# A third SBUF home for projection chunks, loaded ahead of the last stores, and a projection start that waits for one PSUM bank pair at a time

## The chip, the cores and the metric

One core of a Trainium2 chip. A core has TensorE (PE, matrix products), VectorE (DVE), ScalarE (ACT), GpSimd (POOL) and SyncE (SP), which here issues nearly all DMA transfers, in one queue served by 16 DMA engines. The metric is the device time of one execution in microseconds (us), as a median of several.

## What is computed

Four layers in a row on x, of shape 256 x 256 x 64 (tokens by channels). Each layer adds to x the result of a normalised, gated, pairwise contraction:

```python
x = x + layer(_gn(x), ...)              # four times; _gn: group norm with 32 groups
# one layer:
xn = layernorm(x)
left, right = (xn @ Wl + bl) * sigmoid(xn @ Wlg + blg), (xn @ Wr + br) * sigmoid(xn @ Wrg + brg)
out = einsum('bikh,bjkh->bijh', left, right)    # layers 1 and 3 contract over the other axis
out = layernorm(out) * sigmoid(xn @ Wog + bog)  # layers 2 and 3 gate after the last product
return out @ Wo + bo
```

Layers 0 and 2 also multiply left and right by a mask; layer 0 keeps left and right in bf16.

## The kernel before

Layers are numbered 0 to 3. A layer is one block of code in which every engine runs its own list of instructions, and semaphores alone order them. Its stages are `prepare` (a few small products), `norm`, `project` for the first half of the channels, `contract` (`contract_low` in layer 0), `project` for the second half, `contract_kept`, and `finish`. Nothing but semaphores separates one stage from the next, so an engine goes on into the next stage when its own waits allow. SP's transfers are issued strictly in the order of its list: a wait in it holds back all that stands behind it.

**norm.** It handles x as 16 chunks (`NCH`) of 1 MB, two tiles each, so 32 tiles t. For each tile PE centres it into one of three PSUM bank pairs, `banks[t % 3]`, and takes the variance in `banks[3]`; ACT squares it and makes the reciprocal root (logarithm, exponential); DVE scales it (L712, semaphore `normed`) and splits it into a high and a low f16 part (L722, L724, semaphore `lows_ready`). SP stores both parts of chunk n to DRAM (tensor `XH`, or `XHA` in layers 1 and 3) with four transfers of 256 KB each; chunk 14 counts on `stored[0]`, chunk 15 on `stored[1]`.

**project.** It reads the normalised x back in another order, again as 16 chunks c0 to c15 of 1 MB (two transfers of 512 KB, `load_xh_chunk`, L303), and has four SBUF homes for them, one per chunk number modulo 4. All four lie in `kept0`. Home 2 shares its bytes with two of norm's scaled tiles (`yc`), home 3 with one of norm's input chunks; in the second half all four share them with the buffers from which `contract` stores its result. A chunk is handled in eight groups (masked layers 0 and 2) or four units (layers 1 and 3). PE projects into all eight PSUM banks in turn (L802; L812 and L817), ACT takes the sigmoid (L839; L850), in masked layers POOL and DVE multiply the gate by the mask (L865, L886), and DVE multiplies gate and value into the array `LR` (L893; L904, semaphore `products_ready`). PE may be eight groups ahead of DVE's products, not more. Since `LR` also holds the high parts of norm, DVE's first product of the first half waits until chunk 14 is stored:

```python
                if half == 0:
                    dve.wait_ge(stored[0].s, stored[0].n)
                    dve.wait_ge(stored[2].s, stored[2].n)
                    dve.wait_ge(lows_ready.s, lows_ready.n)
```

**contract.** PE contracts in four pieces of four groups; ACT copies each group out of PSUM (`copied`), and SP stores each finished piece to DRAM (tensor `OS`, 2 MB, L1081). Before the store of piece 3 it waits until that of piece 2 has landed, and then issues the second half's c0 and c1. c2 and c3 wait in `project` for the store of piece 3.

Of the kernel before, what the change touches and what calls it, by code (L numbers as in the profile page):

```python
# [48 lines left out]
P = 128  # L49
N = 256  # L50
C = 64
# [52 lines left out]
def build(nc, x_in, masks, consts, params, out):  # L104
    ctx = ExitStack()
    with ctx:
        def sb(name, shape, dt=F32):
            return ctx.enter_context(nc.sbuf_tensor(name, shape, dt))
# [19 lines left out]
        class Arena:  # L128
# [5 lines left out]
            def take(self, cols):  # L134
# [5 lines left out]
        kept0 = sb("kept0", [P, HALF * N])  # L140
        obuf = [kept0[:, i * 16 * 256:(i + 1) * 16 * 256] for i in range(2)]

        xh_b = [[obuf[h // 2][:, at:at + COLS // 2].bitcast(F16) for at in (h % 2 * COLS, h % 2 * COLS + COLS // 2)]
                for h in range(4)]
        squares = [sb(f"squares{i}", [P, 4 * N]) for i in range(2)]

        rings = [[sb(f"{name}s", [P, 2 * BANK])[:, :], square[:, :]] for name, square in zip(("sig", "msg"), squares)]
# [453 lines left out]
        def norm(block, number, layer):  # L601
# [12 lines left out]
            @block.sync  # L614
            def _(sp):
                def store(n, h):
                    sp.wait_ge(lows_ready.s, lows_ready.n + 2 * n + 2)
                    sp.sem_inc(tick.s, 1)
                    for part, v in enumerate((high[h], low[h])):
                        store_xh(sp, n, part, v, k_is_b, stored[h])  # L620

                for h in range(4):
                    sp.wait_ge(stored[h].s, stored[h].n)

                def store_entered(c):
                    sp.dma_start(pair_chunk(XT, c // 8, c % 8), entered(c)).then_inc(stored[2].s, 16)

                load_xt_chunk(sp, 2, 2)
                for n in range(NCH - 1):
                    if n + 3 < from_dram:  # L630
                        sp.wait_ge(centered.s, centered.n + 2 * n + 2)
                        load_xt_chunk(sp, n + 3, n % 3)
                    if n >= 1:
                        store(n - 1, (n - 1) % 2)
                    if from_dram <= n + 2 < NCH:
                        store_entered(n + 2)
                for h in range(2):
                    sp.wait_ge(stored[h].s, stored[h].n + per * (4 if k_is_b else 5))

                load_xh_chunk(sp, 0, 0, k_is_b)  # L640
                store(NCH - 2, 0)
                load_xh_chunk(sp, 1, 1, k_is_b)
                store(NCH - 1, 1)

            @block.tensor
            def _(pe):
                def center(t):
                    n, u = divmod(t, 2)
                    h = n % 3
                    if u == 0 and n < from_dram:  # L650
                        pe.wait_ge(loaded[h].s, loaded[h].n + 16 * (n // 3) + 16)
                    pe.wait_ge(normed.s, normed.n + t - 2)
                    for half in range(2):
                        for s in range(2):
                            rows = slice(C * s, C * s + C)
                            to = banks[t % 3][C * half:C * half + C, s * BANK:(s + 1) * BANK]
                            x = xa[h] if n < from_dram else entered(n)
                            if k_is_b:
                                cols = x[rows, (2 * half + u) * BANK:(2 * half + u + 1) * BANK]
                            else:  # L660
                                cols = x[rows, :].rearrange("p (g j r) -> p j g r", g=8, j=16)[
                                    :, 8 * half + 4 * u:8 * half + 4 * u + 4, :, :]
                            last = pe.matmul(to, cen[rows, rows], cols, start=True, stop=True)  # L663
                    last.then_inc(centered.s, 1)

                def vary(t):
                    pe.wait_ge(squared.s, squared.n + t + 1)
                    pe.wait_ge(logged.s, logged.n + t)
                    for u in range(2):
                        last = pe.matmul(banks[3][:, u * BANK:(u + 1) * BANK], K(K_MEAN),  # L670
                                         sq[t % 3][:, u * BANK:(u + 1) * BANK], start=True, stop=True)
                    last.then_inc(variance.s, 1)

                center(0)
                center(1)
                for t in range(tiles):
                    vary(t)
                    if t + 2 < tiles:
                        center(t + 2)

            @block.scalar
            def _(act):
                def square(t):
                    act.wait_ge(centered.s, centered.n + t + 1)
                    act.wait_ge(variance.s, variance.n + t - 2)
                    act.activation(sq[t % 3], banks[t % 3][:, :], ACT.Square, bias=cb).then_inc(squared.s, 1)  # L686

                def root(t):

# [17 lines left out]
            def _(dve):  # L707
                def scale(t):

                    dve.wait_ge(rooted.s, rooted.n + t + 1)  # L710
                    dve.wait_ge(lows_ready.s, lows_ready.n + t - 3)
                    dve.scalar_tensor_tensor(yc[t % 4], banks[t % 3][:, :], cb, rs[t % 3], ALU.add, ALU.mult).then_inc(normed.s, 1)  # L712

                def halve(t):

# [22 lines left out]
        def project(block, number, layer, half):  # L738
# [21 lines left out]
            def _(sp):  # L760

                if half == 1:
                    sp.wait_ge(stored[1].s, stored[1].n)
                    sp.wait_ge(summed.s, summed.n)
                for h in range(4 if half == 1 and layer["low"] else 2, 4):
                    load_xh_chunk(sp, h, h, k_is_b)
                if half == 0:
                    for h in range(3):
# [7 lines left out]

            @block.tensor
            def _(pe):
                if half == 0:
                    pe.wait_ge(normed.s, normed.n)  # L780
                    pe.wait_ge(logged.s, logged.n)
                else:
                    pe.wait_ge(copied.s, copied.n)
                    pe.wait_ge(copied_v.s, copied_v.n)
                    pe.wait_ge(sums_taken.s, sums_taken.n)
# [8 lines left out]
                with pe.Fori(0, NCH // 4) as i:  # L794
                    for h in range(4):
                        pe.wait_ge(landed[h].s, landed[h].n + 32 * i + 32)
                        if masked:
                            for g in range(8):
                                pe.wait_ge(products_ready.s, products_ready.n + 32 * i + 8 * h + g - 7)
                                for j in range(4):  # L800
                                    for part, w in enumerate((whigh, wlow)):
# [5 lines left out]
                        for two in range(2):  # L807
                            for q in (2 * two, 2 * two + 1):
                                unit = 16 * i + 4 * h + q
                                pe.wait_ge(products_ready.s, products_ready.n + unit - 3)  # L810
                                for s, j in sides_last:
                                    pe.matmul(bank(2 * q + s)[:, j * P:(j + 1) * P], tokens(h, s, q, j, slice(0, P)),  # L812
                                              whigh[:, half * P:(half + 1) * P], start=j == 0, stop=False)
# [165 lines left out]
        def contract(block, number, layer):  # L979
# [89 lines left out]
            def _(sp):  # L1069
                if more:  # L1070
                    load_parameters(sp, number + 1)
                for piece in range(4):
                    ut, cq = divmod(piece, 2)
                    if piece == 3:
# [3 lines left out]
                        for h in range(2):  # L1078
                            load_xh_chunk(sp, h, h, layer["k_is_b"])
                    sp.wait_ge(copied.s, copied.n + 4 * (piece + 1))  # L1080
                    sp.dma_start(OS[ut, :, :, cq, :].rearrange("v p f -> p v f"),  # L1081
                                 hold[piece % 2].rearrange("p (v f) -> p v f", v=16)) \
                        .then_inc(stored[piece % 2].s, 16)
# [684 lines left out]
```

## Time and profile before

| | us |
|---|---|
| median of 3 runs | 2152.24 (2147.28 to 2158.65) |
| profiled execution, time | 2150.95 |
| profiled execution, span | 2148.8 |
| PE busy | 1888.1 (88%) |
| DVE busy | 1693.6 (79%) |
| ACT busy | 1591.5 (74%) |
| POOL busy | 595.4 (28%) |

The span runs from the first to the last instruction in the trace; the time is 2.15 us longer. Busy shares are means over stages with different limits: where an edit touches one place, what counts is which engine or transfer the others wait for at that place. PE's clock has two levels, shown as a granted clock of 1.00 (2.4 GHz) or 0.5 (1.2 GHz).

### The profile page before, as it was taken

To read this page: it belongs to the slowest core of one execution; us is meant where nothing else is said; L and a number is where in the kernel's file an instruction comes from. 1 tells how busy PE (TensorE), PEld (TensorE's weight loads), DVE (VectorE), ACT (ScalarE), POOL (GpSimd) and SP (SyncE) were. 2 spreads that over 40 slices of the span, in tenths; PEclk is the share of its full clock that TensorE was granted. 3 is DMA by queue.
4 is the path that set the end of the run, shared out by engine and by line. 5 is a ranking of instruction groups with operands and counts; after the bars stand their busy time and mean duration, and the time that the engine had idled before them with its cause. 6 is when DMAs were issued, how large, how long until landed. Compare 5 with 4: busy or idle time off the path is not lost. (4 is left out here: it accounts for less than half of the span.)

```text
span 2148.8 us, 44715 instructions
## 1 busy us (share of the span) xinstructions
PE 1888.1 (88%) x14485; PEld 1280.8 (60%) x14492; DVE 1693.6 (79%) x2690; ACT 1591.5 (74%) x2204; POOL 595.4 (28%) x574
## 2 busy tenths in 40 slices
PE   5687979699897998989989799899997879899998
PEld 4423959455422786855622697886552258777665
DVE  6798989989598877688969887878776977677665
ACT  3598969679897756569989775766888966566666
POOL 0001918175100000026400470732870000000755
PEclk8899989999999999999999999999999999999999
DMA  9589938279798739169979954917997993753897
GB/s 393 195 274 312 264 79 235 94 290 384 270 302 275 277 117 312 41 245 402 410 261 316 265 145 150 278 43 278 407 393 256 308 303 130 245 186 127 320 350 299
DMA packets 297397, 549.53 MB, mean 256 GB/s; under 512 B 14768, under 2 KB 170416, under 8 KB 273712
## 3 DMA queue, kind: packets, MB, share of 16 engines
q1 hardware_dynamic: 295680, 538.38, 72.9%
q10 hardware_dynamic: 1584, 9.51, 1.1%
q8 instruction: 68, 1.11, 0.2%
q14 instruction: 65, 0.53, 0.1%
HBM read 371.67 MB, written 176.16 MB: 255 GB/s over the span
## 5 line engine op out<-in xcount | busy, mean ns | idle before, releaser
L1603 POOL TENSOR_TENSOR LR<-LR 128x512 f32<-128x512 f32 x128 | 187.9, 1488 | 523.3 <-DVE LR L1649 501.2
L802 PE MATMUL bank<-whigh,kept 128*128 128x128 f16 x2048 | 268.2, 231 | 30.5 <-DMA kept<-XH 22.5
L1594 POOL TENSOR_TENSOR LR<-LR,sum 128x2048 f32<-128x2048 f32 x30 | 136.5, 4549 | 526.4 <-DVE LR L1408 526.4
L802 PEld LDWEIGHTS bank<-whigh,kept 128*128 128x128 f16 x2048 | 261.5, 150 | 34.6 <-issue 26.3
L802 PE MATMUL bank<-wlow,kept 128*128 128x128 f16 x2048 | 267.4, 230 | 0.0
L802 PEld LDWEIGHTS bank<-wlow,kept 128*128 128x128 f16 x2048 | 261.9, 150 | 0.0
L670 PE MATMUL bank<-LR,kst 128*128 128x512 f32 x512 | 254.3, 619 | 8.3 <-ACT LR L692 6.3
L865 POOL TENSOR_TENSOR msgs<-sigs,mask_sb 128x256 f32<-128x256 f32 x192 | 124.6, 663 | 487.1 <-ACT sigs L839 481.9
L1497 PEld LDWEIGHTS bank<-kst,LR 128*128 128x128 f32 x1024 | 151.0, 192 | 109.9 <-issue 90.7
L1509 PE MATMUL bank<-LR,wog 128*128 128x512 f16 x768 | 211.9, 385 | 4.8 <-ACT msgs L1550 4.0
L670 PEld LDWEIGHTS bank<-LR,kst 128*128 128x128 f32 x512 | 87.6, 191 | 179.1 <-issue 172.9
L812 PE MATMUL bank<-whigh,kept 128*128 128x128 f16 x2048 | 153.4, 226 | 37.1 <-DMA kept<-XHA 32.7
L1007 PE MATMUL bank<-LR 128*128 128x256 f32 x768 | 172.7, 387 | 7.0 <-DVE LR L904 4.2
L1263 PE MATMUL bank<-LR 128*128 128x256 f32 x768 | 169.9, 385 | 7.0 <-DVE LR L904 4.2
L1497 PE MATMUL bank<-kst,LR 128*128 128x128 f32 x1024 | 159.3, 279 | 14.7 <-ACT sigs L1545 7.7
L1007 PEld LDWEIGHTS bank<-LR 128*128 128x128 f32 x768 | 148.6, 194 | 28.3 <-DVE LR L904 4.6
L1263 PEld LDWEIGHTS bank<-LR 128*128 128x128 f32 x768 | 148.0, 193 | 28.2 <-DVE LR L904 4.6
L692 ACT ACTIVATE LR<-bank,epsx 128x1024 f32<-128x1024 f32 x128 | 142.9, 1116 | 25.7 <-PE bank L670 21.6
L812 PEld LDWEIGHTS bank<-whigh,kept 128*128 128x128 f16 x2048 | 121.1, 101 | 64.5 <-issue 36.3
L686 ACT ACTIVATE LR<-bank,small 128x1024 f32<-128x1024 f32 x128 | 140.8, 1100 | 16.5 <-PE bank L663 16.5
L839 ACT ACTIVATE sigs<-bank,small 128x256 f32<-128x256 f32 x256 | 121.1, 478 | 31.8 <-PE bank L802 25.4
L696 ACT ACTIVATE LR<-LR 128x1024 f32<-128x1024 f32 x128 | 135.5, 1058 | 4.0
(189 smaller groups left out, 4106.1 us busy)
## 6 DMA issues: line engine op xcount, KB each, us to landing
LR<-XT SPq DMA_DIRECT2D x103, 1024.0 KB, 8.9
kept<-XH SPq DMA_DIRECT2D x128, 512.0 KB, 5.8
kept<-XHA SPq DMA_DIRECT2D x128, 512.0 KB, 5.1
XT<-LR SPq DMA_DIRECT2D x56, 1024.0 KB, 9.0
LR<-XH SPq DMA_DIRECT2D x64, 512.0 KB, 6.7
LR<-XHA SPq DMA_DIRECT2D x64, 512.0 KB, 6.0
OS<-kept SPq DMA_DIRECT2D x12, 2048.0 KB, 7.5
LR<-OS SPq DMA_DIRECT2D x48, 512.0 KB, 8.5
```

The costliest lines, as they stand in the source:

```text
L670: last = pe.matmul(banks[3][:, u * BANK:(u + 1) * BANK], K(K_MEAN), sq[t % 3][:, u * BANK:(u + 1) * BANK], start=True, stop=True)
L686: act.activation(sq[t % 3], banks[t % 3][:, :], ACT.Square, bias=cb).then_inc(squared.s, 1)
L692: act.activation(lnv[t % 2], banks[3][:, :], ACT.Ln, bias=epsx[:, :], scale=1.0 / X_SCALE ** 2).then_inc(logged.s, 1)
L696: act.activation(rs[t % 3], lnv[t % 2], ACT.Exp, scale=-0.5).then_inc(rooted.s, 1)
L802: last = pe.matmul(bank(g)[:, j * P:(j + 1) * P], tokens(h, g // 4, g % 4, j, slice(0, P)), w[:, half * P:(half + 1) * P], start=part == 0 ...
L812: pe.matmul(bank(2 * q + s)[:, j * P:(j + 1) * P], tokens(h, s, q, j, slice(0, P)), whigh[:, half * P:(half + 1) * P], start=j == 0, stop= ...
L1007: last = pe.matmul(banks[e % 3][:, c * N:(c + 1) * N], src[:, kt, off_a + ch, ut * P:(ut + 1) * P], src[:, kt, off_b + ch, :], start=kt == ...
L1263: last = pe.matmul(banks[e % 3][:, c * N:(c + 1) * N], src[:, kt, off_a + 4 * g + c, ut * P:(ut + 1) * P], src[:, kt, off_b + 4 * g + c, : ...
L1497: last = pe.transpose(by_token(turn_bank(t))[:, :, j, :], n_t[c % len(nrm)][:, :, 4 * q + j], K(K_IDENT))
L1509: last = pe.matmul(bank(2 + t % 2), wog[w][:, :], pair_cols(x, q) if k_is_b else by_b(x, q), start=(w, part) == (0, 0), stop=w == 1)
L1594: pool.tensor_tensor(v, v, token(sum2, c, C), ALU.mult).then_inc(normalized.s, 1)
L1603: pool.tensor_tensor(by_b(x_of(c), q) if end else by_token_cols(x_of(c), q), by_token(gated[t % 4]), by_token_cols(xi[c % len(xi)], q), AL ...
```

## The change

`kept0` keeps homes 0, 1 and 3, and home 2 becomes a buffer of its own, `third_home`, of 8 KB per partition. The room comes from the region set aside for descriptors of dynamic DMAs, which is cut to 1024 bytes per partition. Home 3 takes the bytes that home 2 had.

- At the end of norm, the loads of c0, c1 and c2 are all issued before the stores of chunks 14 and 15. Before, c0 went ahead of the store of chunk 14, c1 between the two stores, and c2 and c3 behind both.
- In contract, c2 of the second half is loaded just before the store of piece 2. c3 alone is left for the place where c2 and c3 stood.
- norm's tiles use `banks[(t + 1) % 3]`, so that the last three tiles end in pairs 0, 1 and 2 in that order, and PE's first projections wait for one pair each (`norm_left`) and no longer for all of norm.

```diff
-        xh_b = [[obuf[h // 2][:, at:at + COLS // 2].bitcast(F16) for at in (h % 2 * COLS, h % 2 * COLS + COLS // 2)]
-                for h in range(4)]
+        xh_homes = [obuf[0][:, 0:COLS], obuf[0][:, COLS:2 * COLS], sb("third_home", [P, COLS])[:, :], obuf[1][:, 0:COLS]]
+        xh_b = [[v[:, at:at + COLS // 2].bitcast(F16) for at in (0, COLS // 2)] for v in xh_homes]
...
-                load_xh_chunk(sp, 0, 0, k_is_b)
+                for h in range(3):
+                    load_xh_chunk(sp, h, h, k_is_b)
                 store(NCH - 2, 0)
-                load_xh_chunk(sp, 1, 1, k_is_b)
                 store(NCH - 1, 1)
...
-                            to = banks[t % 3][C * half:C * half + C, s * BANK:(s + 1) * BANK]
+                            to = banks[(t + 1) % 3][C * half:C * half + C, s * BANK:(s + 1) * BANK]
...
-                for h in range(4 if half == 1 and layer["low"] else 2, 4):
+                for h in range(4 if half == 1 and layer["low"] else 3, 4):
                     load_xh_chunk(sp, h, h, k_is_b)
...
-                if half == 0:
-                    pe.wait_ge(normed.s, normed.n)
-                    pe.wait_ge(logged.s, logged.n)
-                else:
+                def norm_left(h, two_banks):
+                    if half == 0 and h == 0:
+                        if two_banks < 3:
+                            pe.wait_ge(normed.s, normed.n - 2 + two_banks)
+                        else:
+                            pe.wait_ge(logged.s, logged.n)
...
+                                if g % 2 == 0:
+                                    norm_left(h, g // 2)
                                 pe.wait_ge(products_ready.s, products_ready.n + 32 * i + 8 * h + g - 7)
...
                     sp.wait_ge(copied.s, copied.n + 4 * (piece + 1))
+                    if piece == 2:
+                        load_xh_chunk(sp, 2, 2, layer["k_is_b"])
                     sp.dma_start(OS[ut, :, :, cq, :].rearrange("v p f -> p v f"),
...
-    nc = bacc.Bacc("TRN2", target_bir_lowering=False, num_devices=1)
+    nc = bacc.Bacc("TRN2", target_bir_lowering=False, num_devices=1, dynamic_dma_scratch_size=1024)
```

SP's list at the end of norm and the start of the first projection in layer 0, before (`XH<-LR` is the store of chunk 14, `XH<-sum` that of chunk 15, `kept<-XH` a load of half a chunk):

```order
L303 DMA kept<-XH 128x8x256 x2
L277 DMA XH<-LR 64x2x1024 x4
L303 DMA kept<-XH 128x8x256 x2
L277 DMA XH<-sum 64x2x1024 x4
L759 UNCONDITIONAL_BRANCH
L303 DMA kept<-XH 128x8x256 x4
```

The same place after the change:

```order
L303 DMA kept<-XH 128x8x256 x4
L303 DMA third_home<-XH 128x8x256 x2
L277 DMA XH<-LR 64x2x1024 x4
L277 DMA XH<-sum 64x2x1024 x4
L759 UNCONDITIONAL_BRANCH
L303 DMA kept<-XH 128x8x256 x2
```

Four transfers, c1 and c2, moved ahead of the store of chunk 14; the same happens in the other three layers.

SP's list in contract of layer 1, before (`OS<-kept` is the store of a piece):

```order
L1081 DMA OS<-kept 128x16x256 x3
L303 DMA kept<-XHA 128x2x1024 x4
L1081 DMA OS<-kept 128x16x256
L759 UNCONDITIONAL_BRANCH
L303 DMA kept<-XHA 128x2x1024 x4
```

The same place after the change:

```order
L1090 DMA OS<-kept 128x16x256 x2
L303 DMA third_home<-XHA 128x2x1024 x2
L1090 DMA OS<-kept 128x16x256
L303 DMA kept<-XHA 128x2x1024 x4
L1090 DMA OS<-kept 128x16x256
L759 UNCONDITIONAL_BRANCH
L303 DMA kept<-XHA 128x2x1024 x2
```

c2 moved from behind the store of piece 3 to ahead of the store of piece 2.

DVE's list where the first projection of layer 0 begins, before; it is the same after, 7 lines further down in the file:

```order
L724 SCALAR_TENSOR_TENSOR sum<-kept,sum 128x2x512 [waits highs_ready]
L869 UNCONDITIONAL_BRANCH
L876 UNCONDITIONAL_BRANCH [waits lows_ready,stored2,stored0]
L876 ISA
L885 REGISTER_ALU [waits gates_ready]
L886 ISA [waits products_ready]
L886 TENSOR_TENSOR msgs<-sigs,mask_sb 128x256
```

Nothing moved here: the wait for `stored0` still stands ahead of all of DVE's work in the projection.

## Rows read from the trace of the kernel before

**Rows 1.** Waits of PE: line, releaser, total us, times, longest.

```profile
PE bank L812 <- DMA kept<-XHA: 32.7, 7, 7.7
PE bank L802 <- DMA kept<-XH: 22.5, 5, 6.8
```

**Rows 2.** Timeline, norm into projection, layer 0: start, duration, engine, [idle before <- releaser].

```profile
195.95 2.12 SPq L303 DMA_DIRECT2D kept<-XH  x2
...
199.43 3.14 SPq L277 DMA_DIRECT2D XH<-LR  x4
...
199.45 1.28 DVE L712 SCALAR_TENSOR_TENSOR kept<-bank,small,LR 128x1024 f32<-128x1024 f32 x1
...
202.86 0.33 PE L802 MATMUL bank<-whigh,kept 128*128 128x128 f16 x1 [5.69 <-DMA kept<-XH]
202.98 0.31 PE L802 MATMUL bank<-wlow,kept 128*128 128x128 f16 x1
...
206.25 0.42 DVE L886 TENSOR_TENSOR msgs<-sigs,mask_sb 128x256 f32<-128x256 f32 x1 [1.80 <-ACT sigs L839]
...
216.81 0.28 PE L802 MATMUL bank<-whigh,kept 128*128 128x128 f16 x1 [2.69 <-DMA kept<-XH]
...
218.80 0.43 DVE L886 TENSOR_TENSOR msgs<-sigs,mask_sb 128x256 f32<-128x256 f32 x1 [2.58 <-ACT sigs L839]
```

**Rows 3.** Windows: us, busy PE, PEld, DVE, ACT, POOL, PEclk, DMA share, GB/s.

```profile
203.00:217.00 14.00, 10.86 (x131) 10.60 (x132) 9.89 (x22) 7.64 (x16) 7.27 (x12) 0.80 1.01 308
...
224.00:270.00 46.00, 46.00 (x736) 46.00 (x735) 45.66 (x114) 43.80 (x93) 44.17 (x69) 1.00 0.97 249
704.00:745.00 41.00, 40.73 (x792) 33.13 (x787) 34.79 (x51) 31.50 (x50) 0.00 (x0) 1.00 0.90 311
...
830.00:850.00 20.00, 19.95 (x389) 16.28 (x386) 16.89 (x24) 14.96 (x25) 0.00 (x0) 1.00 0.99 352
```

**Rows 4.** Timeline, norm into projection, layer 1.

```profile
690.82 1.41 DVE L904 SCALAR_TENSOR_TENSOR LR<-bank,small,sigs 128x512 f32 x2 [1.37 <-DMA XHA<-LR]
...
695.75 1.89 PE L812 MATMUL bank<-whigh,kept 128*128 128x128 f16 x16 [4.23 <-DMA kept<-XHA]
...
701.05 1.06 PE L812 MATMUL bank<-whigh,kept 128*128 128x128 f16 x16
```

**Rows 5.** Timeline of DVE, first projection of layer 2: first of c0, first of c3.

```profile
1205.89 0.42 DVE L886 TENSOR_TENSOR msgs<-sigs,mask_sb 128x256 f32<-128x256 f32 x1 [2.78 <-ACT sigs L839]
...
1222.73 0.41 DVE L886 TENSOR_TENSOR msgs<-sigs,mask_sb 128x256 f32<-128x256 f32 x1
```

**Rows 6.** Timelines of SP and PE, contract into second projection, layer 1.

```profile
806.21 2.54 SPq L303 DMA_DIRECT2D kept<-XHA  x4
...
821.09 5.91 SPq L303 DMA_DIRECT2D kept<-XHA  x8
...
812.82 1.06 PE L812 MATMUL bank<-whigh,kept 128*128 128x128 f16 x16 [1.42 <-ACT kept L1021]
...
826.66 1.89 PE L812 MATMUL bank<-whigh,kept 128*128 128x128 f16 x16 [6.92 <-DMA kept<-XHA]
...
831.23 1.07 PE L812 MATMUL bank<-whigh,kept 128*128 128x128 f16 x16
...
834.54 1.06 PE L812 MATMUL bank<-whigh,kept 128*128 128x128 f16 x16
```

**Rows 7.** Timelines of SP, PE and DVE, second projection, layer 2.

```profile
1350.89 6.19 SPq L303 DMA_DIRECT2D kept<-XH  x5
...
1357.39 0.33 PE L802 MATMUL bank<-whigh,kept 128*128 128x128 f16 x1 [6.53 <-DMA kept<-XH]
...
1360.09 0.42 DVE L886 TENSOR_TENSOR msgs<-sigs,mask_sb 128x256 f32<-128x256 f32 x1 [6.51 <-ACT sigs L839]
...
1365.64 0.41 DVE L886 TENSOR_TENSOR msgs<-sigs,mask_sb 128x256 f32<-128x256 f32 x1
...
1370.02 0.86 DVE L886 TENSOR_TENSOR msgs<-sigs,mask_sb 128x256 f32<-128x256 f32 x1 [0.28 <-DVE LR L893]
```

More of the change, by code:

```diff
@@ L685, in square @@
                     act.wait_ge(variance.s, variance.n + t - 2)
-                    act.activation(sq[t % 3], banks[t % 3][:, :], ACT.Square, bias=cb).then_inc(squared.s, 1)
+                    act.activation(sq[t % 3], banks[(t + 1) % 3][:, :], ACT.Square, bias=cb).then_inc(squared.s, 1)
                 def root(t):
@@ L711, in scale @@
                     dve.wait_ge(lows_ready.s, lows_ready.n + t - 3)
-                    dve.scalar_tensor_tensor(yc[t % 4], banks[t % 3][:, :], cb, rs[t % 3], ALU.add, ALU.mult).then_inc(normed.s, 1)
+                    dve.scalar_tensor_tensor(yc[t % 4], banks[(t + 1) % 3][:, :], cb, rs[t % 3], ALU.add, ALU.mult).then_inc(normed.s, 1)
                 def halve(t):
@@ L778, in _ @@
             def _(pe):
-                if half == 0:
-                    pe.wait_ge(normed.s, normed.n)
-                    pe.wait_ge(logged.s, logged.n)
-                else:
+                def norm_left(h, two_banks):
[4 more added lines that the diff above has]
+                            pe.wait_ge(logged.s, logged.n)
+                if half == 1:
                     pe.wait_ge(copied.s, copied.n)
@@ L809, in _ @@
                                 unit = 16 * i + 4 * h + q
+                                norm_left(h, q)
                                 pe.wait_ge(products_ready.s, products_ready.n + unit - 3)
```

## The prediction

> **What bounds the kernel now.** I read the waits of PE first, since PE is busy 88% of the span. In two lines PE waits for a chunk of the projection to land: 32.7 us in 7 waits and 22.5 us in 5 [rows 1]. I then looked in the timeline at where these twelve stand. All are in the first few chunks of a projection; further on there are none. There the pace is DVE's in masked layers (45.66 us busy of 46.00, for 736 / 64 = 11.5 chunks, so 4.0 us a chunk) and PE's in the others (40.73 of 41.00) [rows 3]. A projection therefore ends late by what its first chunks lose, and nothing later wins it back. The change touches two sorts of place: the start of the first half's projection (four layers) and of the second half's (layers 1 to 3; layer 0 loads all four chunks ahead already).
>
> The reader is to see one more thing. Where these waits stand, the DMA engines are never idle: share 1.01 at 308 GB/s over the first 14 us of layer 0's projection [rows 3]. Transfers that are issued sooner do not add room there. They only change places with others. So I ask, for each place, who is served later.
>
> **First projection, layer 0.** PE starts c0 at 202.86, when c0 lands (wait of 5.69 us); norm's last L712 began at 199.45 and took 1.28, so it was over at 200.73 [rows 2]. The waits for norm are thus covered by 2.1 us of waiting for c0, whose load keeps its place in SP's list. Waiting for one bank pair at a time gives 0; it would give up to 2.1 us if c0 came sooner, which nothing here brings about. The new order of banks moves no work.
>
> DVE's list has the wait for `stored0` (chunk 14) ahead of everything. In layer 1 the trace names it: DVE's first product, at 690.82, had waited 1.37 us for the store XHA<-LR [rows 4]. In layer 0 the store's four transfers are issued from 199.43 for 3.14 us and DVE starts at 206.25 [rows 2]; the row blames ACT, but it is 3.7 us after the last issue, and I take it to be the same wait. After the change the loads of c1 and c2 stand ahead of that store. Each is 2 x 512 KB = 1.05 MB; at 308 GB/s that is 3.4 us, together 6.8 us. SP's own time to issue them (2.12 us for a chunk [rows 2]) lies beside that. So DVE starts at 206.25 + 6.8 = 213.05. Behind that wait are queued all of DVE's products, behind them PE from the ninth group on (it may be eight ahead), and ACT behind PE. DVE has two chunks to do before c2: 213.05 + 2 x 4.0 = 221.1. Today it starts c2 at 218.80, because c2 landed only for PE's start at 216.81, a wait of 2.69 [rows 2]. The wait for c2 goes, the wait for the store takes its place, and the layer loses **2.3 us**. What is late next is c3: the bytes ahead of it are the same as before, so it lands where it did, one chunk's data behind c2 (about 216.81 + 3.4 = 220.2), and that is before DVE needs it at 225.
>
> **First projection, layer 2.** Same code: 1205.89 + 6.8 + 3 x 4.0 = 1224.7 for the first of c3, against 1222.73 [rows 5]: **+2.0**.
>
> **Layers 1 and 3.** The chunks are read at 352 GB/s [rows 3], 3.0 us each, so DVE starts at 690.82 + 6.0 = 696.8. PE's c1 needs the first product of c0, half of 1.41 us later: 697.5. Today c1 starts when it lands, at 695.75, after a wait of 4.23 [rows 4]. Loss **1.8 us**. c2 starts today with no wait at 701.05, so no further stall is saved. Layer 3 has the same instructions, and I take 1.8 again.
>
> **Second projection, layer 1.** The load of c2 goes ahead of the store of piece 2, and c0 and c1 are issued only when that store has landed: at 806.21 now, at 806.21 + 3.0 = 809.2 then. From issue to PE's start a chunk takes 826.66 - 821.09 = 5.57 us [rows 6], so PE starts c0 at 814.8 and not at 812.82. The long idle time brings the low clock, at which a chunk takes 831.23 - 826.66 = 4.57 us, against 834.54 - 831.23 = 3.31 [rows 6]: PE is through c0, c1 and c2 at 814.8 + 4.57 + 2 x 3.31 = 826.0. The store of piece 3 has the load's 3.0 us ahead of it too, so c3 is issued at 824.1 and starts at 829.7, after a wait of 3.7 us. It starts today at 831.23. But c3 now meets the low clock that c2 met: c4 starts at 829.7 + 4.57 = 834.2 against 834.54. The gain is **0.3 us**, out of a wait of 6.92: the bytes that must land before c3 are the same. Layer 3 (the wait of 7.7 in rows 1): 0.3 again.
>
> **Second projection, layer 2.** Here a chunk load is 3.4 us: c3 is issued at 1350.89 + 3.4 and PE starts it 1357.39 - 1350.89 = 6.5 us later, at 1360.8. DVE follows PE by 1360.09 - 1357.39 = 2.7 us and its first chunk takes 1365.64 - 1360.09 = 5.55 us at the low clock, so c4's first comes at 1369.0, against 1370.02 [rows 7]: gain **1.0 us**.
>
> **The other edits.** The buffer of its own and the smaller scratch region move no instruction, and no transfer here is issued by GpSimd: 0. The four waits of `norm_left` sit in a loop, so they are met in each of its 4 passes; in layers 1 and 3, where PE sets the pace, these are 32. No row has such a wait. PE's instructions start 0.12 us apart at the low clock [rows 2], which bounds it at 32 x 0.12 = 3.8 us; I take 0, since these are no matrix work and PE's queue runs ahead of its array.
>
> **Sum.** 2.3 + 2.0 + 1.8 + 1.8 - 0.3 - 0.3 - 1.0 = **+6.3 us**. Against the profiled execution's own time that is 2150.95 + 6.3 = 2157.3; it lies 1.3 below the median of the runs, and I give the time against the median: **2158.5**.
>
> The price on which all rests is how late two loads make the store. The break-even is a slip of 218.80 - 8.0 - 206.25 = 4.5 us in layer 0 and 695.75 - 0.7 - 690.82 = 4.2 in layer 1; I have 6.8 and 6.0. The slip is bounded below by 0 (the store overtakes) and above by two chunks at 249 GB/s [rows 3], 8.4 us, which adds 1.6 us in layers 0 and 2 and 2.4 in layers 1 and 3: +14.3 in all. In the second projections the low clock may stay away; then layers 1 and 3 gain 4.57 - 3.31 = 1.3 more each and layer 2 5.55 - 4.0 = 1.5 more, and the sum is +2.2.
>
> [...]
>
> **Rivals.**
> - *The low clock takes more (slower).* In layer 0 PE will be through the 64 products of c0 at 202.86 + 64 x 0.12 = 210.5 and idle until DVE's first product at 213.5, 3 us, and much the same in the other first projections. Waits of this size have brought the low clock here (rows 3: granted 0.80 over those 14 us). For layers 0 and 2 I left it out, because DVE has eight groups in hand. If it lasts over c1 and c2, each costs 1.55 more in masked layers (2 x 2 x 1.55 = 6.2) and c2 costs 1.26 more in each of the others (2.5): 6.3 + 8.7 = +15, 2167. It decides (over +10.8) when half of it comes true. Against it: 0.80 over 14 us is 5.6 us at the low level, which c0 alone fills today. 0.17.
> - *The loads and the store share (no change, or a little less).* If store and loads are served side by side and the slip is that of one load, 3.4 or 3.0 us: layer 0 206.25 + 3.4 + 8.0 = 217.65 (-1.1), layer 2 -1.4, layers 1 and 3 690.82 + 3.0 + 0.7 = 694.5 (-1.2 each), with -1.6 in the second projections: -6.5, 2145.7. For it: SP has only one queue but 16 engines, and a transfer waits on the slowest of them. Against it: the engines are full, so sharing makes both late. 0.17.
> - *The change does what it says (faster).* The loads cost nobody anything. First projections: 206.25 + 8.0 = 214.25 (-4.5), 1205.89 + 12.0 = 1217.9 (-4.8), 691.5 for 695.75 (-4.2, twice); second: c3 lands for 826.66, so -3.3 twice, and 1365.64 for 1370.02 (-4.4). Sum -28.7: 2123.5. It needs idle DMA engines, and the rows show none. 0.08.
> - *My forecast:* 0.58, with its own range of 2153 to 2164.
>
> **From these to the numbers.** What a measurement of this kernel can tell from no change is about 0.5%, 10.8 us: below 2141.5 is faster, above 2163.0 slower. Faster: 0.07 of the last rival and a little of the second, 0.09. Slower: 0.14 of the first, 0.06 of the forecast's upper bound, 0.20. Same: 0.71. The range leaves out the fast rival and the outer part of the low-clock one: 2144 to 2168.
>
> **What would show it.** Right: PE's wait at c2 of the first projections is gone; DVE's first product comes about 7 us (layers 0 and 2) and 6 us (1 and 3) later after the end of norm, held by the store of chunk 14; PE waits for DVE at c1. In contract, SP issues c0 and c1 3 us later after the store of piece 2; PE waits about 2 us more at c0, not at c2, and some 3.7 us at c3. PE's c0 in the first projections still waits for its chunk. Wrong: if DVE's first product keeps its distance to norm's end, the slip does not exist and the kernel is faster; if chunks c1 and c2 run at a granted clock of 0.5, it is slower than I say.

## The result, and the profile after

The changed kernel takes **2164.01 us** (median of 5 runs, 2160.9 to 2168.06), the kernel before 2152.24 (2147.28 to 2158.65, now 5 runs). The ratio is 1.0053, with a 95% interval of 1.0032 to 1.0073. So it is 11.4 us slower (from 6.9 to 15.7), where +6.3 was forecast. In the text below a difference is always (ratio - 1) times the median of the kernel before in the same comparison.

The page of the changed kernel, top (engine, busy us, share of the span, instructions) and bytes:

```profile
span 2161.9 us, 44727 instructions
...
PE 1887.9 (87%) x14485; PEld 1281.6 (59%) x14492; DVE 1689.6 (78%) x2690; ACT 1588.7 (73%) x2204; POOL 591.6 (27%) x574
...
DMA packets 297397, 549.53 MB, mean 254 GB/s; under 512 B 14768, under 2 KB 170416, under 8 KB 273712
```

The busy times are those of before within 4 us. No engine has more work; the time went into waits. PE's waits in the projection (line, releaser, total us, times, longest), which answer to [rows 1]:

```profile
PE bank L819 <- DMA kept<-XHA: 29.6, 6, 5.4
...
PE bank L808 <- DMA kept<-XH: 16.8, 3, 6.4
PE bank L808 <- DVE LR L900: 13.5, 6, 5.8
PE bank L819 <- DVE LR L911: 12.3, 3, 6.5
```

Waits for a chunk fell from 55.2 to 46.4 us. Waits for DVE's products, which were 3.7 us in all before, are now 25.8. Nearly all of these stand at c1 of the first projections (5.66, 5.47, 5.77 and 6.50 us in layers 0 to 3).

**First projection, layer 0.** SP, DVE and PE in the timeline (start, duration, engine, [idle before <- releaser]); compare [rows 2]:

```profile
195.54 5.19 SPq L303 DMA_DIRECT2D kept<-XH  x4
200.77 3.68 SPq L303 DMA_DIRECT2D third_home<-XH  x2
204.56 4.28 SPq L277 DMA_DIRECT2D XH<-LR  x4
...
198.89 1.28 DVE L712 SCALAR_TENSOR_TENSOR kept<-bank,small,LR 128x1024 f32<-128x1024 f32 x1
...
213.86 0.43 DVE L893 TENSOR_TENSOR msgs<-sigs,mask_sb 128x256 f32<-128x256 f32 x1 [9.96 <-DMA XH<-LR]
...
202.98 0.32 PE L808 MATMUL bank<-whigh,kept 128*128 128x128 f16 x1 [6.36 <-DMA kept<-XH]
...
214.74 0.32 PE L808 MATMUL bank<-whigh,kept 128*128 128x128 f16 x1 [5.66 <-DVE LR L900]
...
222.22 0.42 DVE L893 TENSOR_TENSOR msgs<-sigs,mask_sb 128x256 f32<-128x256 f32 x1
```

Count from the start of norm's last L712, since the whole trace is shifted by what comes earlier. The store of chunk 14 (`XH<-LR`) is issued 5.67 us after it, where before it was 0.02 us ahead. DVE's first product comes 14.97 us after it, before 6.80: a slip of 8.2 us, and the row now names the store itself. PE still waits for c0's chunk (6.36 us), so waiting for one bank pair at a time won nothing. PE then fills its eight groups and stands 5.66 us for DVE. DVE reaches c2 at 23.33 after L712, before at 19.35 (218.80 - 199.45).

**Layer 1**, the same place:

```profile
691.05 1.28 DVE L712 SCALAR_TENSOR_TENSOR kept<-bank,small,LR 128x1024 f32<-128x1024 f32 x1
...
704.24 1.41 DVE L911 SCALAR_TENSOR_TENSOR LR<-bank,small,sigs 128x512 f32 x2 [8.19 <-DMA XHA<-LR]
...
705.05 1.89 PE L819 MATMUL bank<-whigh,kept 128*128 128x128 f16 x16 [5.47 <-DVE LR L911]
...
710.11 1.07 PE L819 MATMUL bank<-whigh,third_home 128*128 128x128 f16 x16
```

DVE's wait of 1.37 us for the store [rows 4] has become 8.19, and PE's wait of 4.23 us at c1 for its chunk has become one of 5.47 us for DVE. DVE's first product comes 13.19 us after L712 (before 6.38), 14.24 in layer 2 (7.79) and 13.80 in layer 3 (6.63): slips of 6.8, 6.5 and 7.2 us.

**Second projection, layer 1.** Two rows of before that [rows 6] did not need, the start of contract and the stores of pieces 2 and 3:

```profile
749.54 14.08 PE L1007 MATMUL bank<-LR 128*128 128x256 f32 x64 [2.11 <-DVE LR L904]
...
798.68 0.36 SPq L1081 DMA_DIRECT2D OS<-kept  x1
...
812.49 0.37 SPq L1081 DMA_DIRECT2D OS<-kept  x1
```

The same of the changed kernel:

```profile
758.72 14.08 PE L1014 MATMUL bank<-LR 128*128 128x256 f32 x64 [2.11 <-DVE LR L911]
...
807.84 1.23 SPq L303 DMA_DIRECT2D third_home<-XHA  x2
809.12 0.60 SPq L1090 DMA_DIRECT2D OS<-kept  x1
819.73 2.51 SPq L303 DMA_DIRECT2D kept<-XHA  x4
822.28 0.61 SPq L1090 DMA_DIRECT2D OS<-kept  x1
835.46 4.60 SPq L303 DMA_DIRECT2D kept<-XHA  x6
...
825.56 1.89 PE L819 MATMUL bank<-whigh,kept 128*128 128x128 f16 x16 [4.99 <-DMA kept<-XHA]
...
841.87 1.88 PE L819 MATMUL bank<-whigh,kept 128*128 128x128 f16 x16 [4.65 <-DMA kept<-XHA]
...
846.82 1.06 PE L819 MATMUL bank<-whigh,kept 128*128 128x128 f16 x16
```

Counted from the start of contract (749.54, 758.72), with what the prediction's times come to on the same count (its 809.2, 814.8, 824.1, 829.7 and 834.2 less 749.54):

| us from the start of contract | before | predicted | after |
|---|---|---|---|
| store of piece 2 issued | 49.14 | - | 50.40 |
| it has landed: c0, c1 issued | 56.67 | 59.7 | 61.01 |
| PE starts c0 | 63.28 | 65.3 | 66.84 |
| store of piece 3 issued | 62.95 | - | 63.56 |
| it has landed: c3 issued | 71.55 | 74.6 | 76.74 |
| PE starts c3 | 81.69 | 80.2 | 83.15 |
| PE starts c4 | 85.00 | 84.7 | 88.10 |

The reader is to see two things. The store of piece 2 takes 10.61 us from its issue until SP goes on, before 7.53. That is 3.1 more, the 3.0 forecast. But it is also issued 1.26 us later, since SP first issues the two halves of c2 (1.23 us). And the store of piece 3 takes 13.18 us, before 8.60: it now follows c0 and c1 after 2.55 us, before after 6.28, so most of the data of two chunks is still ahead of it. Over the three layers, SP's own waits for these stores rise from 28.5 us (6 waits, the longest 5.8) to 54.8 (6, 11.1).

### The profile page after: what moved, and what is told of

Same layout as the page of the kernel before. It is cut to its first block and busy times, and to the rows that moved or that the text cites. A ratio compares the mean times of both kernels' runs of the same rounds, so it can differ in the third digit from the quotient of the medians.

```text
span 2161.9 us, 44727 instructions
## 1 busy us (share of the span) xinstructions
PE 1887.9 (87%) x14485; PEld 1281.6 (59%) x14492; DVE 1689.6 (78%) x2690; ACT 1588.7 (73%) x2204; POOL 591.6 (27%) x574
## 5 line engine op out<-in xcount | busy, mean ns | idle before, releaser
L808 PE MATMUL bank<-whigh,kept 128*128 128x128 f16 x1536 | 205.7, 233 | 33.5 <-DMA kept<-XH 16.8
L808 PEld LDWEIGHTS bank<-whigh,kept 128*128 128x128 f16 x1536 | 197.7, 150 | 37.3 <-issue 22.6
L808 PE MATMUL bank<-wlow,kept 128*128 128x128 f16 x1536 | 205.0, 232 | 0.0
L808 PEld LDWEIGHTS bank<-wlow,kept 128*128 128x128 f16 x1536 | 198.2, 150 | 0.0
L819 PE MATMUL bank<-whigh,kept 128*128 128x128 f16 x1536 | 120.2, 233 | 43.1 <-DMA kept<-XHA 29.6
L911 DVE SCALAR_TENSOR_TENSOR LR<-bank,small,sigs 128x512 f32 x128 | 90.2, 747 | 57.0 <-ACT sigs L857 39.6
```

Source lines behind the costliest of these rows:

```text
L808: last = pe.matmul(bank(g)[:, j * P:(j + 1) * P], tokens(h, g // 4, g % 4, j, slice(0, P)), w[:, half * P:(half + 1) * P], start=part == 0 ...
```

## The experiments

Nine kernels ran. Theory 1 in all: a store that something waits for is late by the loads issued ahead of it. The rival: the loads cost nothing there, and the time is lost to the low clock or to the new bank order and its waits. All results together (runs of the kernel before in the same comparison: 5 for the change, 11 to 24 for the others):

| run | norm's list | load of c2 in contract | median us | ratio (95%) | difference |
|---|---|---|---|---|---|
| the change | c0 c1 c2 s14 s15 | ahead of store of piece 2 | 2164.01 | 1.0053 (1.0032-1.0073) | +11.4 |
| e1_norm_side | c0 c1 c2 s14 s15 | behind store of piece 3, as before | 2159.88 | 1.0036 (1.0023-1.0049) | +7.7 |
| e2_contract_side | c0 s14 c1 s15 c2 | ahead of store of piece 2 | 2154.99 | 1.0013 (1.0000-1.0025) | +2.8 |
| e6_bank_pairs | c0 s14 c1 s15 c2 | as before | 2153.38 | 1.0001 (0.9991-1.0011) | +0.2 |
| e5_early_c2 | c0 s14 c1 s15 c2 | right behind store of piece 1 | 2143.39 | 0.9961 (0.9948-0.9974) | -8.4 |
| e3_two_after_store | c0 s14 c1 c2 s15 | as before | 2152.00 | 0.9997 (0.9986-1.0008) | -0.6 |
| e4_one_ahead | c0 c1 s14 c2 s15 | as before | 2144.06 | 0.9965 (0.9952-0.9978) | -7.5 |
| e7_both | c0 s14 c1 c2 s15 | right behind store of piece 1 | 2140.71 | 0.9940 (0.9919-0.9961) | -12.9 |
| e9_earlier_c2 | c0 s14 c1 s15 c2 | right behind store of piece 0 | 2141.34 | 0.9947 (0.9927-0.9966) | -11.4 |
| e8_one_ahead_early | c0 c1 s14 c2 s15 | right behind store of piece 1 | 2133.83 | 0.9913 (0.9898-0.9929) | -18.7 |

(s14, s15: stores of chunks 14 and 15. All of these have the third home, the smaller scratch and the rotated banks.)

**e1_norm_side** keeps the change's norm and undoes its contract.

```diff
-                    if piece == 2:
-                        load_xh_chunk(sp, 2, 2, layer["k_is_b"])
...
-                for h in range(4 if half == 1 and layer["low"] else 3, 4):
+                for h in range(4 if half == 1 and layer["low"] else 2 if half == 1 else 3, 4):
```

> The changed kernel with its contract side undone: c0, c1 and c2 of the first projection are still loaded ahead of the stores of chunks 14 and 15, but in contract c2 stands where it stood before, behind the store of piece 3. Store-slip theory: all of the loss of the first projections stays. VectorE's first product comes 13 to 15 us after the start of norm's last scaling (6.4 to 7.8 before), and the kernel is some 10 us slower than before, about 2162. Rival, that the loss is that of the second projections' new order: no slower than before, 2152.

Measured +7.7 us, between +4.9 and +10.5. In layer 0 DVE's first product again waits for the store (start of L712 and first product):

```profile
199.26 1.28 DVE L712 SCALAR_TENSOR_TENSOR kept<-bank,small,LR 128x1024 f32<-128x1024 f32 x1
...
214.72 0.43 DVE L893 TENSOR_TENSOR msgs<-sigs,mask_sb 128x256 f32<-128x256 f32 x1 [10.45 <-DMA XH<-LR]
```

That is 15.46 us after L712. The norm side is most of the loss.

**e2_contract_side** keeps the change's contract and has norm's list as before.

```diff
-                for h in range(3):
-                    load_xh_chunk(sp, h, h, k_is_b)
+                load_xh_chunk(sp, 0, 0, k_is_b)
                 store(NCH - 2, 0)
+                load_xh_chunk(sp, 1, 1, k_is_b)
                 store(NCH - 1, 1)
+                load_xh_chunk(sp, 2, 2, k_is_b)
```

> The changed kernel with its norm side undone: c0, store of 14, c1, store of 15, c2 as before, while in contract c2 is loaded ahead of the store of piece 2. The prediction's term for this side was -1.6 us. By the trace of the changed kernel it is +2.5: the store of piece 2 lands 4.3 us later for layers 1 and 3 (not 3.0), TensorE waits about 5 us at c0 and about 4.5 at c3 of the second projections, and the kernel takes about 2155. If the loads really cost nobody, it is 10 us faster.

Measured +2.8 us (0 to +5.4). Its two halves, 7.7 + 2.8 = 10.5, make up the change's 11.4 within the intervals. In layer 1 SP's list shows the same gaps as in the changed kernel, 10.35 us from the store of piece 2 to c0 and 12.78 from the store of piece 3 to c3:

```profile
805.03 1.23 SPq L303 DMA_DIRECT2D third_home<-XHA  x2
806.30 0.60 SPq L1091 DMA_DIRECT2D OS<-kept  x1
816.65 2.51 SPq L303 DMA_DIRECT2D kept<-XHA  x4
819.21 0.61 SPq L1091 DMA_DIRECT2D OS<-kept  x1
831.99 5.30 SPq L303 DMA_DIRECT2D kept<-XHA  x6
```

**e6_bank_pairs** has both lists of before, and so only the third home, the smaller scratch, the rotated banks and the waits of `norm_left`. Its diff is that of e1 and e2 together.

> Only the buffer of its own, the smaller scratch region, the turned bank order and the waits for one bank pair each; every transfer in its old place. Theory: nothing waits for norm there, since c0 lands 2 us after norm's last scaling, so 0, within 2 us of the kernel before. Rival (the 16 passes with extra waits on TensorE, or the new place of a buffer, cost): several us slower, up to the whole 11.8.

Measured +0.2 us (-1.9 to +2.4). These edits cost nothing and bring nothing, the repeated waits of `norm_left` (bounded at 3.8 us in the prediction) included.

**e5_early_c2** has norm as before, and moves contract's load of c2 from behind the wait for piece 2's copies to ahead of it. SP then issues it right behind the store of piece 1.

```diff
+                    if piece == 2:
+                        load_xh_chunk(sp, 2, 2, layer["k_is_b"])
                     sp.wait_ge(copied.s, copied.n + 4 * (piece + 1))
-                    if piece == 2:
-                        load_xh_chunk(sp, 2, 2, layer["k_is_b"])
```

> As the kernel with only the contract side, but c2 of the second projection is issued one wait sooner, right behind the store of piece 1, where the DMA engines go idle before piece 2 is ready. Theory (what costs is the load's place ahead of a store that is waited for): the store of piece 2 lands 7.5 us after its issue as before, c0 starts as before, c3 is issued directly behind the store of piece 3, TensorE waits about 4 us at c3, and each of the three layers gains 3 to 4.5 us: about 2142. Rival (a low clock and a wait at c3 take the gain back, wherever c2 stands): within 3 us of the kernel before.

Measured -8.4 us: from e2, two lines swapped, and 11.2 us. Layer 1, contract's start, SP, and PE at c0, c3 and c4:

```profile
752.87 13.43 PE L1015 MATMUL bank<-LR 128*128 128x256 f32 x61 [2.11 <-DVE LR L912]
...
786.47 0.37 SPq L1091 DMA_DIRECT2D OS<-kept  x1
786.88 3.38 SPq L303 DMA_DIRECT2D third_home<-XHA  x2
801.99 0.37 SPq L1091 DMA_DIRECT2D OS<-kept  x1
809.53 2.51 SPq L303 DMA_DIRECT2D kept<-XHA  x4
815.80 0.36 SPq L1091 DMA_DIRECT2D OS<-kept  x1
824.35 4.60 SPq L303 DMA_DIRECT2D kept<-XHA  x6
...
816.10 1.06 PE L820 MATMUL bank<-whigh,kept 128*128 128x128 f16 x16 [1.39 <-ACT kept L1029]
...
829.85 1.80 PE L820 MATMUL bank<-whigh,kept 128*128 128x128 f16 x16 [3.55 <-DMA kept<-XHA]
...
834.52 1.06 PE L820 MATMUL bank<-whigh,kept 128*128 128x128 f16 x16
```

The stores take 7.54 and 8.55 us until SP goes on, as before the change (7.53 and 8.60). PE starts c0 as soon as contract's last copy is made (the releaser is ACT, as before), c3 at 76.98 after contract's start where before it was 81.69, and c4 at 81.65 where before it was 85.00. So a home for a third chunk is worth something; it was the place in the list that lost it.

**e9_earlier_c2** issues that load one piece earlier still (`if piece == 1`), right behind the store of piece 0.

> The norm side is as in the kernel before. In the contract section the load of c2 is issued ahead of the wait for piece 1's copies, right behind the store of piece 0, one piece earlier than in the run with the early load. Theory 1 (what the load gains there is only that it is out of the way of the store of piece 2; once it is, earlier is no better): same as that run, -8.4 us, 2143, give or take 2. Theory 2 (how far ahead of the store of piece 2 the load stands still decides, because the transfers between are slow): -11 or better. Theory 3 (it now delays the store of piece 1, which the copies of piece 3 wait for, since the two stores share a buffer): it gives back 3 us or more at the end of contract, -5 or less.

Measured -11.4 us. The intervals of e5 and e9 overlap, so whether the extra 3 us are real, and with it the choice between theories 1 and 2, stays open. Theory 3 (the store of piece 1 becomes the next victim) falls: in layer 1 that store is issued at 787.56, 18 us behind the load (769.56), and for the last 7.5 of them the DMA engines are idle (share 0.01 over 780 to 787.5).

**e3_two_after_store** has contract as before and puts c1 and c2 between the two stores of norm.

```diff
-                for h in range(3):
-                    load_xh_chunk(sp, h, h, k_is_b)
+                load_xh_chunk(sp, 0, 0, k_is_b)
                 store(NCH - 2, 0)
+                load_xh_chunk(sp, 1, 1, k_is_b)
+                load_xh_chunk(sp, 2, 2, k_is_b)
                 store(NCH - 1, 1)
```

> Norm side only, with the order c0, store of 14, c1, c2, store of 15; contract as before. The store that VectorE waits for keeps its place, and c2 overtakes only the store of 15, for which nobody waits in the first three chunks. Store-slip theory: VectorE's first product 6.4 to 7.8 us after the start of norm's last scaling, as in the kernel before; c2 lands some 3 us sooner, and layers 0, 2 and 3 gain 1.5 to 3 us each: about 2144 to 2148. Rival (the store of 15 is also waited for, by the loads from c4 on, and they come late instead): within 2 us of the kernel before.

Measured -0.6 us (-3.0 to +1.7): a miss. The store that DVE waits for is not delayed (DVE waits 1.53 us for it in layer 1, before 1.37), and PE has no wait of 1 us or more for c2 in the first projections, but PE's wait for c1 is still there in layer 1, and behind it c1 runs at the low clock:

```profile
695.75 1.88 PE L820 MATMUL bank<-whigh,kept 128*128 128x128 f16 x16 [3.95 <-DMA kept<-XHA]
...
700.96 1.07 PE L820 MATMUL bank<-whigh,third_home 128*128 128x128 f16 x16
```

```profile
695.70:701.00 5.30, 5.25 (x65) 4.57 (x66) 1.41 (x2) 1.42 (x3) 0.00 (x0) 0.55 1.05 403
```

(The second fence is the window over c1, with the columns of [rows 3].) In layer 1 of the kernel before, in the trace of [rows 4], c2 had no wait that could be won back. New waits also stand at c3: 1.72 us in layer 0 (for DVE) and 1.49 in layer 2 (for the chunk).

**e4_one_ahead** has contract as before and puts only c1 ahead of the store of chunk 14.

```diff
-                for h in range(3):
-                    load_xh_chunk(sp, h, h, k_is_b)
+                load_xh_chunk(sp, 0, 0, k_is_b)
+                load_xh_chunk(sp, 1, 1, k_is_b)
                 store(NCH - 2, 0)
+                load_xh_chunk(sp, 2, 2, k_is_b)
                 store(NCH - 1, 1)
```

> Norm side only, with one load more ahead of the store of 14 instead of two: c0, c1, store of 14, c2, store of 15. Store-slip theory: the slip is half of that of the change, 3 to 4 us (VectorE's first product 10 to 11.5 us after the start of norm's last scaling), which is just under the break-even of 4.5 and 4.2 us, so the time is near the kernel before, -3 to +2 us. If the loss grows with the number of moved loads and not with a threshold, it is half of what two loads cost, +4 us: 2156.

Measured -7.5 us (-10.3 to -4.7), better than either theory had it. DVE's first product slips by 4.2, 3.0, 3.2 and 2.7 us in the four layers (10.96, 9.38, 11.00 and 9.30 after L712), so one load costs half of what two do, and each slip stays below the break-even of 4.5 or 4.2 us that the prediction worked out. In layer 1 PE's waits at c1 fall from 4.23 to 1.31 us, and c1 then runs at the full clock:

```profile
689.38 1.28 DVE L713 SCALAR_TENSOR_TENSOR kept<-bank,small,LR 128x1024 f32<-128x1024 f32 x1
...
698.76 1.41 DVE L912 SCALAR_TENSOR_TENSOR LR<-bank,small,sigs 128x512 f32 x2 [4.38 <-DMA XHA<-LR]
...
699.57 1.28 PE L820 MATMUL bank<-whigh,kept 128*128 128x128 f16 x16 [1.31 <-DVE LR L912]
...
702.88 1.28 PE L820 MATMUL bank<-whigh,third_home 128*128 128x128 f16 x16
```

```profile
699.50:704.50 5.00, 4.86 (x96) 4.00 (x96) 4.29 (x8) 2.54 (x4) 0.00 (x0) 1.00 1.05 397
```

c1 takes 3.31 us from start to start, in e3 5.21 and in the change 5.06. The profiled execution of e3 took 2144.72 us and that of e4 2151.72, the other way round from their medians, so the traces show the places and the medians the totals.

**e7_both** is e3's norm with e5's contract.

> Both orders that keep clear of a store that is waited for: c0, store of 14, c1, c2, store of 15 at the end of norm, and c2 of the second projection issued right behind the store of piece 1. If the two are independent, the gains add: 8.4 us of the early c2 and 4 to 8 of the other, about 2136 to 2140. If both give the same wait back to something later (a pace that another engine sets), less than either sum: above 2142.

Measured -12.9 us (-17.4 to -8.4). The time, 2140.71, lies between the two that were expected. e3's -0.6 and e5's -8.4 make -9.0: they add up within the interval, though only just.

**e8_one_ahead_early** is e4's norm with e5's contract.

> The norm side of the run with one load ahead (c0, c1, store of chunk 14, c2, store of chunk 15), which alone gave -7.5 us, and the contract side of the run with the early load of c2 (issued right behind the store of piece 1, before the wait for the copies of piece 2), which alone gave -8.4. They lie at different places of the program. Theory 1 (a place gains what its own first waits lose, and places add up): -7.5 - 8.4 = -15.9 us, 2136, ratio 0.9926. Theory 2 (the pace of DVE or PE in the rest of the projection takes part of it back): no better than the better of the two, about -9, 2143. Between the two, at -12.5, neither is borne out. In the profile under theory 1: DVE's first product about 3 us later after norm than in the kernel before, no wait of PE at c2 of the first projections, and no wait of over 2 us at c3 of the second ones.

Measured -18.7 us (-22.0 to -15.3), where adding gives -15.9 and theory 2 about -9. The places add up. One sign did not come: PE was to wait no more than 2 us at c3 of the second projections, and it waits 3.45 us in layer 1 and 3.79 in layer 3 (1.86 in layer 2), as in e5 (3.55 in layer 1). This kernel beats both others: 2133.83 us, with the same bytes and the same work.

## Why the prediction was right or wrong

The time lies in the range (2144 to 2168) and at the upper edge of the forecast's own (2153 to 2164). At +11.4 us it is just over the 10.8 from which the prediction speaks of "slower" (it gave that 0.20, and 0.71 to "no change"); the interval, 6.9 to 15.7, reaches to both sides. The direction, the places and the mechanism of the first projections came as forecast. One term, that of the second projections, had the wrong sign: -1.6 us forecast, +2.8 to +4.4 measured.

To see which, one must not compare single executions alone: a stretch of the same code differs by 2 to 4 us between two of them. So I took, from the profiled execution of each kernel, two stretches per layer: from the last L712 to contract's first matmul (the first projection), and from that to the first matmul of the second half's contract (the second projection). The mean of the kernels with the old list is set against those with the change's list and the better ones:

| stretch | layer 0 | layer 1 | layer 2 | layer 3 | sum of differences |
|---|---|---|---|---|---|
| first projection, list of before (5 kernels) | 78.6 | 66.1 | 78.0 | 66.2 | |
| change's list (2: the change, e1) | +2.0 | +1.9 | +1.4 | +2.0 | +7.2 |
| c0 s14 c1 c2 s15 (2: e3, e7) | -1.4 | -0.5 | -0.7 | -1.0 | -3.6 |
| c0 c1 s14 c2 s15 (2: e4, e8) | -1.3 | -2.3 | -0.2 | -2.0 | -5.9 |
| second projection, list of before (5) | | 127.6 | 141.0 | 122.2 | |
| change's list (2: the change, e2) | | +3.8 | -2.2 | +2.8 | +4.4 |
| c2 early (4: e5, e7, e8, e9) | | -3.1 | -6.3 | -3.4 | -12.8 |

**First projections (+7.9 forecast): the mechanism right, the number with some luck.** +7.2 in the table, +7.7 in e1. DVE's `stored0` wait took the place of c2's, PE waits for DVE at c1, and c0's chunk still starts the projection. The slips (8.2, 6.8, 6.5, 7.2) are in three layers larger than the forecast ones (6.8, 6.0, 6.8, 6.0). In layer 0 it all but reaches the upper bound of 8.4: SP's issuing does not lie beside the data as I had it, for the six loads take 5.19 + 3.68 = 8.87 us to issue where c0's two took 2.12, and the store is issued behind that. Against the one trace that I costed from, the four stretches of the changed kernel grew by 3.8, 2.6, 1.9 and 2.6 us, 10.8 in all, about what the larger slips give (7.9 + 3.0). That trace is 4.0 us shorter in these stretches than the mean of the five (in layer 0 76.61, mean 78.6), and only so does 7.2 come out beside 7.9: that nearness is luck. Nor does "c2 starts today with no wait" hold in every execution: in layer 1 of e6 and e9, which have norm's old list, PE waits 3.27 and 3.22 us for c2; in e2 and e5 it does not.

The Trainium skill, "DMA: Bandwidth & Descriptors", section "Where 436 GB/s comes from", gives 435 GB/s for the ports of SBUF and says that between HBM and SBUF the HBM side binds, at about 358 GB/s for a core. By the 358, two chunks would take 5.9 us (an estimate from the page's figure). The traces agree with neither figure as a price: two loads made the first product later by 6.5 to 8.2 us, while windows of 5 us with loads and stores together moved 397 and 403 GB/s (e4 and e3, above). Another section of that page, "Two DMAs through the same engine are not ordered", says that transfers of one queue start in order within a DMA engine but are pipelined. The traces agree with the order: what waits for the store of chunk 14 is later by all of the loads ahead of it, in layer 0 4.2 us by one chunk and 8.2 by two.

**Second projections (-1.6 forecast): wrong, +4.4 in the table and +2.8 in e2.** The step that failed is "the store of piece 3 has the load's 3.0 us ahead of it too" in layers 1 and 3. What stands ahead of that store is not c2, which had landed by then, but c0 and c1. These are issued only when the store of piece 2 has landed. Before, that was 6.28 us ahead of the store of piece 3; now it is 2.55 us, because piece 3's copies did not move and piece 2's store did. The store of piece 3 therefore waits 4.58 us more, not 3.0. The second miss is small and was there to be read: SP's 1.26 us to issue c2 stand ahead of the store of piece 2. Together, 1.26 + 3.08 - 3.73 (the slack between the loads and the next store that absorbs part of it) + 4.58 = 5.19 us later for c3's issue (76.74 - 71.55), where the prediction had 74.6 - 71.55 = 3.0. In layer 2 the gain is there (-2.2, forecast -1.0), but kernels with the old list differ by 4.6 us among themselves in this stretch (138.3 to 142.9).

**The rivals.** "The low clock takes more" came true in its mechanism and not in its price. In all four layers PE's new wait at c1 brings the low level; windows over it in layers 0 and 1 (PEclk is the third number from the end; it is 0.66 over 1224 to 1229 and 0.52 over 1754 to 1761, in layers 2 and 3):

```profile
211.00:218.00 7.00, 3.26 (x32) 3.27 (x33) 4.14 (x11) 1.32 (x3) 0.61 (x1) 0.51 0.94 275
702.00:710.00 8.00, 4.95 (x64) 4.45 (x64) 4.14 (x6) 1.27 (x3) 0.00 (x0) 0.57 0.93 330
```

But in layer 0 DVE goes from its first product to c2 in 222.22 - 213.86 = 8.36 us, not the 8.0 of the full clock: 0.4 us lost and not 3.1, since DVE has eight finished groups to work on while PE is slow. In layer 1 c1 ran at the low clock before the change too. "The loads and the store share" falls by the slips. "The change does what it says" falls with its norm half, but what it said of contract is what e5 does: it had c3 start at 77.12 us after contract's start (826.66 - 749.54), and in e5 c3 starts at 76.98. The prediction held against this rival that the rows show no idle DMA engines. Those rows stand over projections. In contract the trace of before has idle ones, ahead of the stores of pieces 1 and 2 in layer 1 (columns of [rows 3]; the DMA share is the last number but one):

```profile
775.00:784.00 9.00, 7.92 (x38) 6.66 (x37) 6.15 (x10) 5.26 (x6) 0.00 (x0) 1.00 0.01 2
790.00:798.60 8.60, 8.60 (x42) 7.57 (x41) 6.26 (x15) 5.15 (x5) 0.00 (x0) 1.00 0.02 6
```

The change issues c2 just after the second of these, when piece 2 is ready; e5 issues it ahead of it.

**What gives e4 and e8 their gain** is argued from places, and partly shown. Where the load of c1 goes ahead of one store, PE's wait at c1 becomes short and the low clock stays away in layer 1. The clock is not all of it: in layer 3 the stretch is 2.0 us shorter too, though waits of 1.57 us (e4) and 1.87 (e8) at c1 are followed there by the low level in the second half of c1 (granted 0.68 over 1747.5 to 1752 and over 1728 to 1733). Why e3, which in the table gains 3.6 us, shows only -0.6 in 12 runs stays open; two traces of it are too few.

## What to carry to other kernels

A load issued earlier on a busy queue is paid by whatever stands behind it. Ask who waits for that store, and compare the slip (data of the load, plus the time to issue it) with the slack of the wait that it would relieve: here one load ahead was under the break-even and won, two were over it and lost. If a load's buffer has been free for long, put it where the queue's next item is far off, such as ahead of SP's own wait for an engine: in contract that was a swap of two lines and 11 us. And when a transfer slips, look at the gap to the next item behind it, for a chain of "store, loads, store" closes up.

## What was not expected of the hardware

- SP's time to issue a load is not fixed. Two halves of a chunk took 1.23 us in layer 1 of the changed kernel (807.84), 3.68 in layer 0 (200.77) and 3.38 in e5 (786.88), right behind a store of 2 MB.
- A wait of PE of 3.95 us brought the low clock behind it (granted 0.55, the 1.2 GHz level for most of it) and one of 1.31 us did not (granted 1.00, 2.4 GHz). In one chunk that is 5.21 against 3.31 us: 1.9 us on top of the wait. No length of wait that decides it comes out of these runs: waits of 1.57 and 1.87 us in layer 3 were followed by 0.68.
- Single windows with loads and stores together moved 397 and 403 GB/s in layer 1, more than the 352 from which the chunks were priced; the slips there (3.0 for one, 6.8 for two) do not show that rate.
